# Cross attention on one core: key projections as three products of rounded parts, context split by GpSimd, projections in other slots

## What is computed

```python
x = x + attn(layernorm(x))                      # token and channel diffusion, 16 and 8 heads
x = x + xattn(layernorm(x), ctx_1024)           # the part that is changed
x = x + moe(layernorm(x))                       # 8 experts, 2 picked per token

def xattn(query, value):                        # value: 16 x 1500 x 128, 16 heads of depth 8
    q = split_heads(query @ wq.T + bq)
    k = split_heads(value @ wk.T + bk)
    v = split_heads(value @ wv.T + bv)
    attn = softmax(einsum('bhqd,bhkd->bhqk', q, k) / sqrt(8))
    return merge_heads(einsum('bhqk,bhkd->bhqd', attn, v)) @ wo.T + bo
```

## Time and profile before

| | us |
|---|---|
| median of 3 runs | 630.91 (628.44 to 633.17) |
| the profiled execution's own time | 632.53 |
| its span in the trace | 630.3 |
| TensorE busy in the span | 584.3 (93%) |
| VectorE busy | 460.3 (73%) |
| ScalarE busy | 380.1 (60%) |
| GpSimd busy | 215.7 (34%) |

### The profile page before, as it was taken

How to read it: one execution, slowest core, us unless ns; L and a number is a source line. 1 busy time by engine, 2 the same in 40 slices (tenths; PEclk the granted TensorE clock), 3 DMA queues, 4 the chain that set the end, 5 groups by cost and what they waited for, 6 DMA issues and landing times.

```text
span 630.3 us, 17326 instructions
## 1 busy us (share of the span) xinstructions
PE 584.3 (93%) x6542; PEld 465.9 (74%) x6542; DVE 460.3 (73%) x850; ACT 380.1 (60%) x602; POOL 215.7 (34%) x185
## 2 busy tenths in 40 slices
PE   3699787798999999999999999999999989999997
PEld 1566464476778778778777787877888768999985
DVE  4865456866887887887887887887787467676676
ACT  2457455265665665665665665665656676667762
POOL 4575324722242242242232232232221224433430
PEclk9889899799999999999999999999999999999999
DMA  5000005499266366366366366367380101211000
GB/s 219 1 3 3 0 2 119 86 192 210 77 148 147 99 146 151 93 146 156 88 146 162 88 141 166 88 137 172 79 197 3 51 1 60 73 62 57 1 0 34
DMA packets 25286, 59.91 MB, mean 95 GB/s; under 512 B 14104, under 2 KB 14488, under 8 KB 25248
## 3 DMA queue, kind: packets, MB, share of 16 engines
q1 hardware_dynamic: 25248, 59.38, 39.5%
HBM read 20.49 MB, written 0.52 MB: 33 GB/s over the span
## 4 chain that ended last, share of the span: by engine, by line
PE 68%; SPq 7%; ACT 3%; issue 3%; DVE 2%; DMA 1%; ACTq 0%; DVEq 0%
PE PS L1739 12%; PE PS L1723 12%; PE PS L1699 11%; PE PS L1869 6%; PE PS L225 6%; PE PS L1871 6%; PE PS L1870 5%; PE PS L217 5%; SPq L1080 3%; SPq L1073 3%; PE PS L1755 3%; ACT k_full L246 1%; SPq L1088 1%; DMA q_stack<-neg_rows 1%; PE PS L1709 1%
## 5 line engine op out<-in xcount | busy, mean ns | idle before, releaser
L1427 DVE TENSOR_REDUCE chunk_max<-PS 128x1 f32<-128x500 f32 x336 | 214.3, 673 | 60.8 <-PE PS L1699 59.2
L1268 ACT ACTIVATE P<-PS 125x896 f32<-125x896 f32 x192 | 173.5, 914 | 122.0 <-PE PS L1723 121.1
L1699 PE MATMUL PS<-k_hi,q_block_hi 128*128 128x500 f32 x336 | 131.2, 439 | 6.3 <-ACT k_full L246 3.3
L1723 PE MATMUL PS<-q_stack,k_stack 97*125 97x224 f32 x768 | 122.7, 283 | 3.3 <-DMA q_stack<-neg_rows 2.0
L1723 PEld LDWEIGHTS PS<-q_stack,k_stack 97*125 97x125 f32 x768 | 107.0, 190 | 18.2 <-issue 8.0
L255 POOL TENSOR_TENSOR k_lo<-k_full,k_hi 128x500 fp32r<-128x500 f32 x48 | 61.2, 1278 | 103.6 <-ACT k_full L246 101.3
L1699 PEld LDWEIGHTS PS<-k_hi,q_block_hi 128*128 128x128 f32 x336 | 61.0, 193 | 36.8 <-ACT k_full L246 16.7
L1739 PE MATMUL PS<-P,values 125*32 125x112 f32 x3072 | 83.6, 260 | 0.5 <-ACT P L1268 0.5
L1739 PEld LDWEIGHTS PS<-P,values 125*32 125x32 f32 x3072 | 72.0, 110 | 13.9 <-issue 10.7
L1161 POOL TENSOR_TENSOR q_stack<-q_copies,consts 96x896 fp32r<-96x896 f32 x16 | 26.9, 1678 | 132.0 <-PE PS L1723 131.6
L1592 DVE TENSOR_TENSOR PS<-gated,PS 128x448 f32<-128x448 f32 x64 | 40.2, 628 | 30.5 <-PE PS L1871 28.6
(11 more groups left out here) (192 smaller groups left out, 892.8 us busy)
## 6 DMA issues: line engine op xcount, KB each, us to landing
k_stack<-k_hi SPq DMA_DIRECT2D x128, 187.5 KB, 4.5
ctxT<-ctx_in SPq DMA_DIRECT2D x16, 750.0 KB, 4.4
k_stack<-k_lo SPq DMA_DIRECT2D x64, 187.5 KB, 4.5
w_gate_up<-wgu_in SPq DMA_DIRECT2D x8, 512.0 KB, 3.6
w_down<-wd_in SPq DMA_DIRECT2D x8, 256.0 KB, 3.7
q_stack<-neg_rows SPq DMA_DIRECT2D x112, 0.5 KB
mats<-mats_in SPq DMA_DIRECT2D x1, 832.0 KB, 5.6
q_copies<-q_hi SPq DMA_DIRECT2D x8, 98.0 KB, 4.6
```

The lines of the kernel that those rows point to most:

```text
L1268: nc.scalar.activation(P[:, t % RING, :].rearrange("p (a n) -> p a n", a=2), PS[0:KR, 2 * (t % 2):2 * (t % 2) + 2, 0:HALF], ACT.Exp).then_ ...
L1427: nc.vector.tensor_reduce(out=chunk_max[:, n // KC, n % KC:n % KC + 1], in_=PS[:, max_bank(b, n), 0:KW], axis=AX.X, op=ALU.max).then_inc(m ...
L1699: nc.tensor.matmul(PS[:, max_bank(b, n), 0:KW], q_block_hi[:, j, 128 * t:128 * t + 128], k_hi[:, j, KW * c:KW * c + KW], start=True, stop= ...
L1723: last = nc.tensor.matmul(PS[0:KR, 2 * (t % 2) + g // 2, o:o + GH * N], k_stack[:, j, g, KR * t:KR * t + KR], q_stack[0:SHIFT_ROW + 1, j, ...
```

## The change

The key products of batches 2 to 15 are no longer float32 matmuls. The weights wk are split once into a rounded part wk_hi (ScalarE) and the rest wk_lo (VectorE). The context of a batch is split by GpSimd into ctx_hi and ctx_lo, 1500 columns each, at the end of the period before the one that uses it; batch 2 is split ahead of the loop. A key product is then three matmuls of rounded parts: hi x hi, hi x lo, lo x hi. Keys move from slots 2, 3, 4 to 5, 6, 7, values from 1, 6, 7 to 1, 2, 4. To make room, the matrices of the first stage get a tensor of their own that is freed, and are loaded by a DMA of their own; ctx_hi and ctx_lo lie where the experts' weights come later, so SP waits for the last key product before it loads these.

```diff
-                    sp.dma_start(mats[:, :, :], mats_in).then_inc(weights_loaded, 16)
+                    sp.dma_start(mats1[:, :, :], mats_in[:, 0:S1_MATS, :]).then_inc(weights_loaded, 16)
+                    sp.dma_start(mats[:, :, :], mats_in[:, S1_MATS:, :]).then_inc(weights_loaded, 16)
...
+            ctx_hi = until_experts.enter_context(nc.sbuf_tensor("ctx_hi", [128, S], F32R))
+            ctx_lo = until_experts.enter_context(nc.sbuf_tensor("ctx_lo", [128, S], F32R))
...
-            KEY_SLOTS, VALUE_SLOTS, TURN_SLOTS = [2, 3, 4], [1, 6, 7], [3, 8]
+            KEY_SLOTS, VALUE_SLOTS, TURN_SLOTS = [5, 6, 7], [1, 2, 4], [3, 8]
...
                         if isinstance(b, int) and b == B - 3:
+                            sp.wait_ge(k_projected, KC * B)
                             for e in range(2):
                                 load_gate_up(sp, e, e)
...
+                    def split_context(b, j, u):
+
+                        pool.wait_ge(ctx_loaded[j], 16 * (u + 1))
+                        if later(b, 3):
+                            pool.wait_ge(k_projected, KC * b)
+                        nc.gpsimd.tensor_tensor(ctx_hi[:, :], ctxT[:, j, :], C["ones"][:, 0:1].broadcast_to([128, S]), ALU.mult
+                                                ).then_inc(ctx_rounded, 1)
+                        pool.wait_ge(ctx_rounded, b - 1)
+                        nc.gpsimd.tensor_tensor(ctx_lo[:, :], ctxT[:, j, :], ctx_hi[:, :].bitcast(F32), ALU.subtract
+                                                ).then_inc(ctx_split, 1)
+
...
                             split_keys(pool, b + 2, j, u + 1)
+                        if exists(b + 3, B):
+                            split_context(b + 3, 1 - j, u + 1 if j == 0 else u + 2)
...
+                    split_context(2, 0, 1)
                     pipelined(pool, period, B)
...
+                    nc.scalar.copy(wk_hi[:, :], MAT["wk"]).then_inc(wk_split, 1)
                     read_keys(act, 1, 1, 0, 0, FIRST_KEY_BANKS[0])
...
+                    dve.wait_ge(wk_split, 1)
+                    nc.vector.tensor_tensor(wk_lo[:, :], MAT["wk"], wk_hi[:, :].bitcast(F32), ALU.subtract).then_inc(wk_split, 1)
                     take_chunks(0, 0, range(QT7 * KC))
...
                                 take_bank(BANK_OF["key", c], (k_ready, KC * (b + 2) + c + 1))
-                                project_keys(pe, b + 2, j, u + 1, c, bank("key", c))
+                                if c == 0:
+                                    pe.wait_ge(ctx_split, b + 1)
+                                k = slice(KW * c, KW * c + KW)
+                                three_passes(bank("key", c)[:, 0:KW], wk_hi[:, :], wk_lo[:, :], ctx_hi[:, k], ctx_lo[:, k]
+                                             ).then_inc(k_projected, 1)
```

More of the change, by code:

```diff
@@ L40 @@
 MATS = ["Wqk_t", "Wv_t", "Wo_t", "Wqk_c", "Wv_c", "Wo_c", "wq", "wk", "wv", "wo0", "wo1", "wo2", "wo3"]
+S1_MATS = 6
 ROWS = ["gamma1", "gamma2", "bv", "bo"]
@@ L95, in build @@
         X = sb("X", [128, PAIRS, D])
-        mats = sb("mats", [128, len(MATS), D])
+        mats = sb("mats", [128, len(MATS) - S1_MATS, D])
         rows = sb("rows", [128, len(ROWS), D])
@@ L100, in build @@
         consts = sb("consts", [128, consts_in.shape[1]])
-        MAT = {n: mats[:, k, :] for k, n in enumerate(MATS)}
+        MAT = {n: mats[:, k, :] for k, n in enumerate(MATS[S1_MATS:])}
         ROW = {n: rows[:, k, :] for k, n in enumerate(ROWS)}
@@ L281, in build @@
         with s1:
+            mats1 = sb1("mats1", [128, S1_MATS, D])
+            MAT.update({n: mats1[:, k, :] for k, n in enumerate(MATS[:S1_MATS])})
             Z = sb1("Z", [128, PAIRS, D])
@@ L582, in _ @@
                     shift(1, 1)
-                    dve.wait_ge(weights_loaded, 32)
+                    dve.wait_ge(weights_loaded, 48)
                     nc.vector.tensor_tensor(wo_scaled[:, 0, :], MAT["Wo_t"], ROW["gamma1"], ALU.mult
@@ L669, in _ @@
                     turn_tokens(0)
-                    pe.wait_ge(weights_loaded, 32)
+                    pe.wait_ge(weights_loaded, 48)
                     for c in range(2):
@@ L817, in _ @@
                     project_values(pe, 0, 0, 0, 2, SPARE)
+        with ExitStack() as until_experts:
+            ctx_hi = until_experts.enter_context(nc.sbuf_tensor("ctx_hi", [128, S], F32R))
+            ctx_lo = until_experts.enter_context(nc.sbuf_tensor("ctx_lo", [128, S], F32R))
         w_gate_up = sb("w_gate_up", [128, 2, 2 * I])
@@ L900, in build @@
             q_block_hi = sb2("q_block_hi", [128, 2, HQ], F32R)
+            wk_hi = sb2("wk_hi", [128, D], F32R)
+            wk_lo = sb2("wk_lo", [128, D], F32R)
             q_copies = sb2("q_copies", [SHIFT_ROW, GROUPS, B, N], F32R)
@@ L1049, in build @@
             x2_ready = sem("x2_ready")
+            wk_split = sem("wk_split")
+            ctx_rounded = sem("ctx_rounded")
+            ctx_split = sem("ctx_split")
             TURN_REST, PROJECT_REST = 8, 12
@@ L1749, in denominators, with three_passes @@
                                          ).then_inc(den_done, 1)
+                    def three_passes(bank_, hi, lo, moving_hi, moving_lo, start=True, stop=True, **more):
+                        nc.tensor.matmul(bank_, hi, moving_hi, start=start, stop=False, **more)
+                        nc.tensor.matmul(bank_, hi, moving_lo, start=False, stop=False, **more)
+                        return nc.tensor.matmul(bank_, lo, moving_hi, start=False, stop=stop, **more)
                     def project_out(b, j):
@@ L1773, in _ @@
                     pe.wait_ge(ones_loaded, 16)
+                    pe.wait_ge(wk_split, 2)
                     def turn_group(g):
@@ L1866, in _ @@
                     pipelined(pe, period, B)
[L1868 to L1871, removed]
                     def gates(e, j, k):
```

## The result

The median went from 630.97 us (7 runs) to 625.03 us (7 runs, 622.57 to 626.35): a ratio of 0.990, 95% interval 0.987 to 0.992. The forecast was 629.0 (620 to 637), so the time is in the range, 4.0 us under the value, and the gain, 5.9 us, is three times the one predicted. At 1.0% it lies on the border between my "within 1%" and "faster".

A forecast was written before the change was run, and what follows sets the result against it. TensorE's fixed order bounds it: 22.7 us a period plus 0.7 of bank waits. Products -0.48, old waits -0.71, new waits +1.07: -0.12 a period, thirteen times -1.6, with 0.3 at the loop's start -1.9, from 630.91 to 629.0 us (620 to 637).

The forecast's parts named there:

- Three products: Key products on TensorE: three rounded passes cost 0.69 us instead of 0.85, saving 0.48 us a period.
- The old waits: TensorE's bank waits in slots 3 and 4 (0.38 and 0.13, plus two tenths) go: 0.71 us a period.
- (a): Slot 8: the second transpose waits 0.5 us for key product 2's bank, read by ScalarE, plus a tenth.
- (b): Slot 5: key product 0 waits 0.2 us for the bank of values 2, read by VectorE, plus a tenth.
- (c): Slot 3: the first transpose waits 0.07 us for the bank of maximum 13, plus a tenth.
- The scaling of the heads: VectorE, slot 4: with GpSimd idle there, the scaling takes 0.39 us instead of 1482 ns.
- The split: GpSimd's two context operations take 6.6 us a period, hidden with 7.6 us of cover before slot 5 needs them.
- Ends of the loop: Outside the thirteen periods: 0.3 us gained at period 1's start; period 14 moves by half a microsecond at most.
- Rival 1: Banks: the new waits don't occur and only the removals count, 15.5 us gained, 615 us; chance 0.17.
- Rival 2: Bank readers: waits by whole durations, (a) 0.95, (b) 0.5, (c) 0.2; +0.75 a period, 640 us; chance 0.12.
- Rival 3: GpSimd's split runs into slot 4 and holds up the scaling of the heads; +30 us, 660; chance 0.03.
- Rival 4: Key products: rounded passes cost 0.28 us each, so nothing is saved; +0.4 a period, 636 us; chance 0.06.

The follow-up runs named there:

- e2: The changed kernel with the old slots (keys 2, 3, 4; values 1, 6, 7); ratio 0.996 to the kernel before.
- e4: The changed kernel without the third pass (wk_lo x ctx_hi) of each key product; ratio 0.984 to the kernel before.
- e5: The changed kernel with GpSimd's subtraction into ctx_lo repeated once more; ratio 0.993 to the kernel before.
- e6: The changed kernel with GpSimd's subtraction into ctx_lo repeated three times more; ratio 1.091 to the kernel before.
- e1: The kernel before with only the slots changed (keys 5, 6, 7; values 1, 2, 4), float32 products, no split; 630.35 us, ratio 0.996.
- e3: The changed kernel with keys in slots 3, 5, 7, values still in 1, 2, 4; ratio 0.986 to the kernel before.
- e8: The changed kernel with the second transpose in slot 9 instead of 8; median 630.8 us, ratio 0.999 to the kernel before.
- e7: The changed kernel with keys in slots 3, 5, 7 and values in 1, 4, 6; ratio 0.988 to the kernel before.
- e11: The changed kernel unaltered, measured again; 626.84 us, ratio 0.991 to the kernel before.

## Why the prediction was right, and where its numbers were off

**What bounds it.** Right. TensorE's fixed order with waits at banks fits the runs in kind: of the work removed, e2 gives back two fifths as waiting and e4 seven tenths, e5 adds GpSimd work at no cost in the period, and e6 costs as soon as the cover is spent. In size the walk was less good: the periods of e1, e2, e3 and e8 fell outside what I expected of them. And that the time is within the range says little, for the range is 17 us wide and the gain was three times the one forecast.

**Three products.** 0.68 against 0.69 each; -0.51 a period instead of -0.48.

**The old waits.** The maximum of slot 3 no longer waits, and e1 gives the net of the trade. Right.

**The new waits: the step that failed is the size of (a), "It waits 0.5".** The wait is there, at that matmul and for that reader, but it is 0.32, and the tenth that I put behind it isn't there (327.20 to 327.29, 0.09, for a transpose of 0.12): together about 0.3 too much, of the 0.37 by which the period was misjudged. The term of the chain that was too large is "key 1 is there at 0.68 + 1.05": I had 1.73 from the scores of slot 6 to k_hi, and it is 1.54. ScalarE's timeline after:

```profile
323.05 0.92 ACT L1296 ACTIVATE P<-PS 125x896 f32<-125x896 f32 x1 [1.12 <-PE PS L1753]
323.96 0.68 ACT L246 ACTIVATE k_hi<-PS,cols 128x500 fp32r<-128x500 f32 x1
...
325.09 0.92 ACT L1296 ACTIVATE P<-PS 125x896 f32<-125x896 f32 x1
```

Key product 1 starts at 323.08, 0.66 behind the scores (0.68 forecast), and k_hi starts 0.88 behind it and not 1.05. The chain of waits above goes from its last pass straight to k_hi. From there on the walk holds: two readings take 1.13 (1.14), the next exponential starts at 2.67 instead of 2.87, and the whole chain ends at 4.78 instead of 4.96; TensorE's side was 4.46 for 4.43. The 1.05 came from key product 0 in the kernel before, 319.74 to 320.93, 1.19. Key product 1 of the same period, which starts at 322.57, has 1.03 to its k_hi:

```profile
323.60 0.68 ACT L245 ACTIVATE k_hi<-PS,cols 128x500 fp32r<-128x500 f32 x1 [0.56 <-PE PS L217]
```

That distance is 1.03 or 1.04 in ten of the twelve middle periods, and less the 0.16 by which a product got lighter it would have given 0.87. With 1.04 in that place the same walk gives e1, whose products are the float32 ones, a wait of 0.20 (0.68 + 1.04 + 3.23 against 4.43 + 0.32), and 0.18 was measured. Why the reading of product 0 comes 0.16 later the traces don't show. The exponential, too, starts earlier than I had it, 0.63 behind its scores and not 0.79, which I had taken from scores whose record is 0.68 long instead of 0.60; but in the walk it ended at 1.59, ahead of the 1.73, so that alone changed nothing. Such a wait is a small difference of two large sums, and 0.17 in one offset is a third of the 0.5.

(b) and (c) were forecast as 0.2 and 0.07 with a tenth each. By start distances key product 0 waits 0.03 (319.27 to 319.54, for 0.24), and to the weighing behind it there are 0.88 for 0.68 of passes; the rest is a tenth or two that lies in places where no wait is named. The first part of the period has 0.1 less than forecast for both.

**The scaling of the heads.** 0.39, as forecast. The Trainium skill (SBUF — State Buffer, "Who interferes with whom") says that a VectorE instruction with two SBUF inputs contends with a GpSimd instruction that reads SBUF, and that the port pair that they share is an exclusive lock. The traces agree: 393 and 391 ns in the changed kernel and e1, where GpSimd is idle, against 1322 in the median of e2, where the keys are back in slots 2 to 4, and 2022 in e6. In these two the scaling ends 0.25 us behind GpSimd's operation.

**The split.** 6.1 us against 6.6, cover 7.9 against 7.6; e6 measured the cover directly. "Gone only if the two take over 14 together": right. The one place without cover is the entry (e2, e5, e7).

**Ends of the loop.** The first period had 0.4 more than the later ones before and is no longer than them after; with its own 0.49 that makes the 0.96 of the table. I had 0.3 for it. The last periods moved by 0.1.

**Rivals.** Rival 1 (615 us, no new waits) fails: the wait of (a) stands in the trace, and e3, which removes it, gains. Rival 2 (waits by whole durations) fails by sign: its (a) was 0.95. Rival 3 didn't occur: the next scaling of the heads is at 343.26, 8.6 us behind the end of the split and 5.4 behind that of blocks (336.21 + 1.69). In e6, with 10.2 us more, the scaling is held up as this rival has it, but the wait that costs is the key product's. Rival 4: passes are 0.23, not 0.28.

**In the sum.** -0.49 instead of -0.12 a period, thirteen times, is 4.8 us; the entry lost 0.2 that I had not forecast, and the first period gained 0.1 more. That is the distance from 629.0 to 625.0, with 0.7 between the profiled pair and the medians.

## What to carry to other kernels

Where an engine runs a fixed order through rotating banks, work removed from it is worth only what isn't given back at the next bank whose reader is late: take the readers' chain and the engine's chain up to that point, and expect only a part of the removal (here 0.30 of 0.51, 0.21 of 0.69) unless the readers are spaced out too. Such a wait is the difference of two sums of 4 to 5 us, so read every offset from more than one instance of the row (here 1.19 and 1.03 in one period), with the same neighbours where there is one, and give the difference an uncertainty of two tenths, which times the number of periods is the width of the forecast. Divide a profiled pair into stretches by the same event before reading a gain: here 1.4 of 7.9 us were the first stage's own scatter.

## What the hardware showed that I had not expected

The first attention, the same instructions in the changed kernel and in e2 to e11, took in eleven profiled executions from 106.8 us (e2) to 110.2 us (e7), and 112.8 in e8, up to the first q copy: more than the whole effect of one of the parts. The granted clock up to 106 us goes with it: 0.95 to 0.97 in the four that came there before 108.1 us, 0.92 to 0.94 in the five between 108.9 and 109.7, 0.90 in e7 and 0.87 in e8. What sets the clock differently there I haven't traced.

In e6, where TensorE waits 2.5 us in each period, the mean granted clock over the loop is 0.94, between the two levels (1.2 and 2.4 GHz), and the weighing right behind the wait takes 1.2 us more, most of it at the lower level (granted clock 0.57). In the wait itself (332 to 335 us) the clock is still 1.00; it falls behind it and is back at 1.00 from 340 us on. Being late cost 1.6 times the wait.

GpSimd's longer operations are a little better than their length: 3.41 us for 1500 elements against 1.26 for 500 of the same kind (2.7 times), and 2.69 for the product with a broadcast operand. The float32 product of two passes takes 0.83 to 0.85 us, three passes of rounded operands 0.68.
